# One exponential ahead of each group's scores, and the softmax sums folded and spread by one transfer each

## The reference

```python
def _L1_xattn_ref(hidden_q, kv_c, Wq, w_kc_q, w_kc_kv, W_qr, W_kr, Wo):
    q_hk = (hidden_q @ Wq.T).reshape(Bv, Sv, H, K)
    q_big = jnp.einsum('bshk,hkq->bshq', q_hk, w_kc_q)
    q_big = _apply_rope(q_big, sin_q[None, :, None, :], cos_q[None, :, None, :])
    kv_r = _apply_rope(kv_c, sin_k[None], cos_k[None])
    q_r = jnp.einsum('bshq,hqr->bhsr', q_big, W_qr)
    k_r = jnp.einsum('bld,hdr->bhlr', kv_r, W_kr)
    scores = jnp.einsum('bhsr,bhlr->bhsl', q_r, k_r)
    attn = jax.nn.softmax(scores, axis=-1)
    ctx_c = jnp.einsum('bhsl,bld->bhsd', attn, kv_r)
    ctx_lat = jnp.einsum('bhsd,hkd->bhsk', ctx_c, w_kc_kv)
    ctx = ctx_lat.transpose(0, 2, 1, 3).reshape(Bv, Sv, H * K)
    return ctx @ Wo.T
...
x = x + jnp.tanh(g_xattn[0]) * _L0_xattn_ref(_layernorm(x, axis=-1), ctx_512, ...)
x = x + jnp.tanh(g_ffn[0]) * _L0_ffn_ref(_layernorm(x, axis=-1), ...)
x = x + jnp.tanh(g_xattn[1]) * _L1_xattn_ref(_layernorm(x, axis=-1), ctx_512, ...)
x = x + jnp.tanh(g_ffn[1]) * _L1_ffn_ref(_layernorm(x, axis=-1), ...)
```

## Time and profile before

| | us |
|---|---|
| median of three runs | 3444.43 (3439.39 to 3446.43) |
| the profiled execution | 3444.42 |
| its span, first to last instruction | 3442.4 |
| TensorE busy (weight loads beside it) | 3002.3, 87% of the span (2002.3) |
| VectorE busy | 2327.0, 68% |
| GpSimd busy | 1559.6, 45% |
| ScalarE busy | 1338.1, 39% |

### The profile page before, as it was taken

One profiled execution on the slowest core, in us unless ns is written; L12 is line 12 of the kernel. 1 busy time (PEld: TensorE's weight loads), 2 busy tenths in 40 slices (PEclk: granted clock), 3 DMA queues, 4 the chain that ended last, 5 costly groups with the idle time before them and its releaser, 6 DMA issues. The chain is left out here.

```text
span 3442.4 us, 55921 instructions
## 1 busy us (share of the span) xinstructions
PE 3002.3 (87%) x16656; PEld 2002.3 (58%) x16656; DVE 2327.0 (68%) x3226; ACT 1338.1 (39%) x2810; POOL 1559.6 (45%) x1035
## 2 busy tenths in 40 slices
PE   6999979999699999999999999999999999997344
PEld 4777779999555555565565565555556556554123
DVE  5777754544676676676676667658667667766787
ACT  1323322222244444434434444444443443443456
POOL 0000022222355555555565465556465556553566
PEclk9889979999799999999999999999999999999566
DMA  4000010000200000000000000000000000010100
GB/s 107 0 0 0 0 49 6 10 10 23 59 13 21 17 16 15 22 9 22 15 15 18 20 18 16 19 18 16 15 20 11 22 15 15 10 47 13 60 14 23
DMA packets 130212, 70.65 MB, mean 21 GB/s; under 512 B 83582, under 2 KB 124510, under 8 KB 129880
## 3 DMA queue, kind: packets, MB, share of 16 engines
q1 hardware_dynamic: 129944, 67.45, 7.8%
HBM read 56.95 MB, written 10.04 MB: 19 GB/s over the span
## 5 line engine op out<-in xcount | busy, mean ns | idle before, releaser
L1102 POOL TENSOR_TENSOR c_psum<-c_p 120x800 f32<-120x800 f32 (+1 forms) x384 | 750.8, 1961 | 779.0 <-ACT c_p L1350 463.7
L1163 DVE TENSOR_REDUCE c_mneg<-c_m_ps 128x1 fp32r<-128x1452 f32 (+1 forms) x448 | 744.8, 1662 | 412.6 <-PE c_m_ps L1394 412.4
L1350 ACT ACTIVATE c_p<-c_s_ps 120x400 f32<-120x400 f32 (+1 forms) x1536 | 655.2, 509 | 772.5 <-PE c_s_ps L1477 770.0
L1490 PE MATMUL c_o_ps<-c_p,c_val 120*64 120x400 f32 (+1 forms) x3072 | 598.8, 512 | 5.7 <-DVE c_q L1193 5.7
L1476 PE MATMUL c_s_ps<-c_q,c_k 128*120 128x400 f32 (+1 forms) x1536 | 569.3, 371 | 12.4 <-issue 5.7
L1477 PE MATMUL c_s_ps<-c_q,c_k 128*120 128x400 f32 (+1 forms) x1536 | 529.9, 345 | 0.0
L1394 PE MATMUL c_m_ps<-c_k,c_q 64*128 64x484 f32 (+1 forms) x1344 | 323.9, 439 | 99.9 <-DVE c_mneg L1163 70.8
L1476 PEld LDWEIGHTS c_s_ps<-c_q,c_k 128*120 128x120 f32 (+1 forms) x1536 | 278.9, 182 | 171.6 <-issue 158.8
L1093 POOL TENSOR_TENSOR l_rr<-c_psum,l_rr 96x400 f32<-96x400 f32 x256 | 260.8, 1040 | 210.7 <-DVE l_rr L1206 210.6
L1490 PEld LDWEIGHTS c_o_ps<-c_p,c_val 120*64 120x64 f32 (+1 forms) x3072 | 187.0, 136 | 281.2 <-issue 139.0
L1431 PE MATMUL c_s_ps<-c_xt,l_a 128*96 128x400 f32 x1536 | 309.5, 351 | 1.9 <-DVE c_xt L1151 1.9
(11 more groups left out here) (232 smaller groups left out, 4157.4 us busy)
## 6 DMA issues: line engine op xcount, KB each, us to landing
c_rdb<-l_denominators SPq DMA_DIRECT2D x128, 100.0 KB, 2.7
c_kv<-in_ctx SPq DMA_DIRECT2D x32, 360.0 KB
c_q<-c_mneg SPq DMA_DIRECT2D x384, 0.5 KB, 1.9
c_den<-c_oden SPq DMA_DIRECT2D x256, 0.8 KB
x_rows<-in_x SPq DMA_DIRECT2D x4, 800.0 KB
x_spill<-x_rows SPq DMA_DIRECT2D x8, 400.0 KB
l_xa<-x_spill SPq DMA_DIRECT2D x8, 400.0 KB
c_xr<-x_spill SPq DMA_DIRECT2D x32, 100.0 KB
```

Source lines behind the costliest of these rows:

```text
L1102: g.tensor_tensor(psum[0:k, u % 2, :], p[0:k, 2 * u % 4, :], p[0:k, (2 * u + 1) % 4, :], ALU.add).then_inc(psum_ready, 1)
L1163: v.tensor_reduce(mneg[0:n, c, t:t + 1], m_ps[0:n, :, 0:4 * KP], AX.XY, ALU.max, negate=True).then_inc(mneg_ready, 1)
L1350: a.activation(p[0:k, w % 4, i * HALFQ:(i + 1) * HALFQ], s_ps[0:k, (2 * w + i) % 4, 0:HALFQ], ACT.Exp).then_inc(exp_ready, 1)
L1490: mm = pe.matmul(o_ps[i * DL:(i + 1) * DL, 0:HALFQ], val[0:k, j % 2, r, :], p[0:k, w % 4, i * HALFQ:(i + 1) * HALFQ], start=(r == 0), stop ...
```

## The change

Three edits, all in `phase_l1_attention`.

- At the start of ScalarE's list of each group's body an exponential of one number is taken, from the identity matrix into a new tile `c_warm` of 1 x 1. It waits for nothing.
- The fold is one transfer in place of four. It reads the four rows (partitions 0, 32, 64, 96) and writes 100 partitions x 8 numbers: 100 pieces of 8 numbers on either side.
- The spread is one transfer in place of two. It reads 2 halves x 64 copies x 400 numbers, and writes 128 partitions x 400 numbers.

The semaphores' thresholds follow: a transfer adds 16, so `den_loaded` counts by 16 for a chain and not by 64, `rdb_loaded` by 16 and not by 32.

```diff
+        warm = sb("c_warm", [1, 1])
...
                     sp.wait_ge(od_ready, PRIMED + ch + 1)
-                    for i in range(4):
-                        sp.dma_start(den[i * S // 4:(i + 1) * S // 4, :], oden[32 * i:32 * i + 1, :].rearrange("o (p f) -> o p f", p=S // 4)).then_inc(den_loaded, 16)
+                    sp.dma_start(den[:], oden[0:128:32, :].rearrange("o (p f) -> o p f", p=S // 4)).then_inc(den_loaded, 16)
                     sp.wait_ge(rden_ready, PRIMED + ch + 1)
                     sp.dma_start(io["den"].rearrange("(p f) -> p f", p=S), rden[:]).then_inc(rdb_row, 16)
                     sp.wait_ge(rdb_row, 16 * (ch + 1))
                     sp.wait_ge(ct_ready, PRIMED + ch)
-                    for i in range(2):
-                        sp.dma_start(rdb[i * DL:(i + 1) * DL, :], io["den"][i * HALFQ:(i + 1) * HALFQ].partition_broadcast(DL)).then_inc(rdb_loaded, 16)
+                    sp.dma_start(rdb[:], io["den"].rearrange("(i n) -> i n", i=2).unsqueeze(1).broadcast_to((2, DL, HALFQ))).then_inc(rdb_loaded, 16)
...
                 def invert(ch):
-                    v.wait_ge(den_loaded, 64 * (ch + 1))
+                    v.wait_ge(den_loaded, 16 * (ch + 1))
...
                 def normalise(ch, c):
-                    v.wait_ge(rdb_loaded, 32 * (ch + 1))
+                    v.wait_ge(rdb_loaded, 16 * (ch + 1))
...
                 def drain_sums(ch):
                     a.wait_ge(den_done, PRIMED + ch + 1)
-                    a.wait_ge(den_loaded, 64 * ch)
+                    a.wait_ge(den_loaded, 16 * ch)
...
                 def group(it):
+                    a.activation(warm[:], m.ident[0:1, 0:1], ACT.Exp)
                     for u, j, c, q in pairs():
```

## The result

The changed kernel takes 3579.69 us (median of four runs, 3575.66 to 3592.11), the kernel before 3445.43 us on the same occasion (3439.39 to 3449.17). The ratio is 1.0397, 95% interval 1.0368 to 1.0427: **slower by 134 us**. The forecast was slower by 70 us, at 3514 us, with a range up to 3565. The direction and the mechanism held, the size did not.

What follows compares the result with a forecast made beforehand. TensorE, busy 2109.71 us of the second attention layer's 2290, was taken as the bound; only its pauses count. Terms 36.8 + 2.4 + 6.7 + 4.2 + 2.3 + 19.2 - 1.9 = 69.7 us gave 3514 us, range 3465 to 3565.

Steps and rivals of the forecast that it cites:

- Two engines: In the merged spread: the source's outer count of 2 leaves two DMA engines, landing 6.2 us after issue; chance 0.80.
- the first rival: In the spread: the destination's 128 rows decide, sixteen engines share it, landing 2.7 us after issue; 3427 us, chance 0.09.
- The price of a piece: In the spread's transfer: each 1,600-byte piece costs 0.07 us, with bounds 0.048 and 0.080 from a weight load.
- The third rival: In the spread: two engines at 0.080 us a piece, 3560 us, or 3575 with other transfers' pieces; chance 0.06.
- The keys: TensorE's keys in batches 1 and 2: normalisation and queued row maximum 2.3 us late in 16 places, costing 36.8 us.
- The chains in chunk 1: Chunk-0 chains of batches 0 to 2, run in chunk 1: late maximum and row cost 0.1 us in 24, 2.4 us.
- the credit of 0.4 us for the fold: In those 24 chains run in chunk 1: earlier sums shorten TensorE's 0.52 us pause for the row maximum by 0.4 us.
- The group's last chunk: Batch 3's chunk-0 chain in seven groups: 2.7 us more waiting, mostly swallowed; 0.95 us each, 6.7 us.
- The clock: TensorE after the 16 pauses at the keys: half pace for 3.4 us loses 1.2 us each (at most 1.7), 19.2 us.
- The exponential: ScalarE's table load at each group's first scores moves into a wait: 0.32 us gained in six groups, -1.9 us.
- the chain of batch 3: Batch 3's chunk-1 chain, finished in the next head: spread late on VectorE, 0.6 us in each of 7 heads, 4.2 us.
- the project: TensorE's project in batch 3, 8 places: 2.3 us of cover hides the late maximum, cost nothing; any excess counts eight times.

Runs made afterwards that it cites:

- The run with the maximum first: The changed kernel, spread still one transfer, but VectorE takes the row maximum before the normalisation and TensorE's last project waits for the normalisation: 3464.9 us, ratio 1.0054.
- the idle spread: The kernel before plus an unneeded one-transfer spread into a free tile in the 24 chunk-1 chains of batches 0 to 2: 3463.43 us, ratio 1.0047.

## Why the prediction was right in kind and half in size

**Two engines: right.** 130 packets for a spread, 104 for a fold, and two transfers by columns no better. The Trainium skill, page "DMA: Bandwidth & Descriptors", section "Why a DMA increments its semaphore by 16 and not by 1", which says that both sides' slowest dimensions count, agrees with each of these; the first rival, which took the destination's rows, fell.

**The price of a piece: wrong by a fifth.** "I take 0.07, measured on these very pieces" was the step. The spread of the changed kernel kept its engines busy for 8.5% x 16 x 7.4 us = 10.1 us, 0.079 us a piece, and its two lists lasted 5.5 us, 0.086 us a piece with their holes. The normalisation started 7.29 us after the issue (2700.94 to 2708.23) where I had 6.2. The bound of 0.080 from the weight load was nearer than the same pieces on sixteen engines, and I had treated a list as if it ran without holes. The third rival, with longer lists and 3560 to 3575 us, had this part and came nearest to the 3579.69 measured, though I gave it 0.06.

**The keys: right place, and a size that is part luck.** 2.3 us in 16 places, measured (62.4 - 19.5) / 16 = 2.7. Two errors nearly cancelled. VectorE's new wait is 3.41 us (at 2552.19 above) and not 2.3, as the spread is 1.1 us longer. But the normalisation itself, which I had left at its 1.66 us, took 0.77: 3.41 + 0.77 - 1.66 = 2.5 us. In the kernel before GpSimd was busy during the whole of that normalisation, as the fifth busy time of this window shows:

```profile
1609.25:1610.91 1.66, 1.53 (x9) 0.62 (x11) 1.66 (x3) 0.64 (x2) 1.66 (x2) 1.00 0.07 1
```

In the changed kernel VectorE came to it later, beside less of GpSimd's work (0.34 of the 0.77 us); over all 64 its mean fell from 1143 ns to 639. That GpSimd's work is the cause was not tested.

**The chains in chunk 1: wrong by a factor of ten.** I charged 0.1 us each, 2.4 in all, and they cost 26.4. The path I named was right (the maximum late, its row late, the first scores waiting), but two terms of the step fell: the spread is 1.1 us later than I had it, and the credit of 0.4 us for the fold does not exist. Over the 24 chains the maximum starts 1.7 us later against TensorE's work than before, where I had 1.0, and 1.1 us of that reaches the scores where I let 0.1 through; even the upper bound of 1.0 each was passed.

**The group's last chunk: wrong.** I let idle time and 0.44 us of slack swallow most of 2.7 us and took 0.95 us. The wait for the spread grew by 3.8 us where I had 2.7 (3.96 in the earlier trace rows, some 7.7 now), and 18.2 + 8.1 = 26.3 us arrived, some 3.6 us in each of seven groups and 1 us in the last: almost none was swallowed. The run with the maximum first leaves this part unchanged, so it is a path of its own.

**The clock: wrong by more than two.** I took 16 x 1.2 = 19.2 us with 1.7 as the most. TensorE's busy time grew by 45.9 us, and 42 of it went away with the pauses at the keys and the first scores. The pauses near 1 us don't do it: with the idle spread, 24 waits for a row of 0.9 us on average left TensorE at 2110.79 us. So some 42 / 16 = 2.6 us follow each pause of 3.6 us. The step that failed took the length of the half-paced stretch, 3.4 us, from the single example in the earlier trace rows, and the bound of 1.7 us with it. In the changed kernel's trace the clock stood at the lower level for 88.8 us around the ends of these sixteen pauses, 3.4 to 6.8 us each and 5.5 on average, of which some 75 us lay beside running products: at half pace 37 of the 42 us. One of the long ones:

```profile
1053.90:1060.70 6.80, 6.13 (x24) 4.88 (x26) 4.27 (x6) 4.30 (x9) 0.00 (x0) 0.50 0.18 55
```

The price is no constant: in the kernel with the spread alone the same sixteen pauses came with 61.4 us at the lower level. I had also misread the stage before, whose pauses I put at about 1 us at most: at its two ends they are longer, 5.5 us for its last output product (L1407 above).

**The rest: small.** The exponential gave 3.2 us instead of 1.9 in the rows, the fold's earlier sums nothing that TensorE felt. At the stage's end 8.9 - 5.5 = 3.4 us came instead of 2.3. In the head the chain of batch 3 cost nothing (4.2 forecast), in batch 3 the project paid 6.2 - 2.5 = 3.7 us (0 forecast, with the remark that an excess would count).

Together: 42.9 + 26.4 + 26.3 + 7.3 + 45.9 less some 3 us, where I had 69.7. The largest parts of the miss are the clock (45.9 where I had 19.2), the chains in chunk 1 (26.4 for 2.4) and the group's last chunk (26.3 for 6.7). The price of a piece lies under the last two, as it makes every wait 1.1 us longer; the rest is the fold's credit in the chains, and at the last chunk idle time that I counted on and that was not there.

## What to carry to other kernels

Before transfers are merged, look at the outermost count of both access patterns: a broadcast of two rows is one transfer less and fourteen engines fewer. When a transfer gets slower, ask what stands behind the waiting instruction in its engine's list; here one independent instruction moved ahead of the wait won back 115 of 134 us, and 10 us in the kernel before the change. A small saving can be worth nothing in one kernel and, by the rows, some 33 us beside another fault, as the fold was: undo edits one at a time in both directions.

## What the runs showed of the hardware that I had not expected

The two engines' lists didn't run evenly: in the spread alone in its window they moved mostly 9 to 43 GB/s in the first half and 52 GB/s towards the end, with one fetch of instructions as the only other traffic in the window. Why is open. And a small transfer that is issued behind 64 pieces on two engines lands late, 3.5 instead of 1.7 us for a row of 32 numbers 4.9 us behind the idle spread, and 5.1 us for a row of 128 numbers 1.5 us behind the real one.
